# A graph network on one core: no memset between the scatters, and six of a tile's 13 layer-1 products between the groups of the next tile's aggregation

## The reference

```python
edge_index = jnp.stack([src, dst])
h = relu(layernorm(x));  x = x + L0(h, src, dst)
h = relu(layernorm(x));  x = x + L1(h, edge_index, edge_weight)

def L0(feat, W1, W2, b, src, dst):
    t1 = feat @ W1
    msg = t1[src] + feat[src] * feat[dst] @ W2
    scale = sqrt(out_deg[src]) * sqrt(out_deg[dst])
    agg = segment_sum(msg / scale[:, None], dst)
    embed = leaky_relu(where(in_cnt > 0, t1 + agg, 0) + b, 0.01)
    return embed / max(norm(embed), 1e-12)

def L1(h, edge_index, ew, W, b, W1, b1, W2, b2):
    # self-loops added; norm = dinv[row] * ew * dinv[col]
    h7 = segment_sum((h @ W)[col] * norm, row) + b
    return relu(h7 @ W1 + b1) @ W2 + b2
```

## Time and profile before

| | us |
|---|---|
| median of 3 runs | 2632.22 (2628.5 to 2633.63) |
| the profiled execution | 2630.78 |
| its span in the profile | 2628.8 |
| first scatter starts | 58.75 |
| last scatter starts | 1203.41 |
| layer 0's last step ends, about | 1754 |

### The profile page before, as it was taken

How to read it: one execution, slowest core, us unless ns; L and a number is a source line. 1 busy time by engine, 2 the same in 40 slices (tenths; PEclk the granted TensorE clock), 3 DMA queues, 4 the chain that set the end, 5 groups by cost and what they waited for, 6 DMA issues and landing times. The chain is left out here.

```text
span 2628.8 us, 22584 instructions
## 1 busy us (share of the span) xinstructions
PE 1912.9 (73%) x7229; PEld 1164.1 (44%) x7239; DVE 1340.5 (51%) x1970; ACT 483.5 (18%) x636; POOL 955.0 (36%) x1107
## 2 busy tenths in 40 slices
PE   5599477773211122113999999999998999999996
PEld 1388122551100011002777676757788534443443
DVE  7878588231000000002454545555665878787886
ACT  1000200331000000000555455534102400000000
POOL 2888888887777777772000000000000400000000
PEclk9755798886555555555999999999999999999998
DMA  7788600433002000010675767641774355565663
GB/s 287 313 337 331 239 8 8 143 109 101 1 1 88 1 13 1 26 62 13 230 268 215 269 217 272 224 167 53 261 231 132 102 154 164 166 182 156 176 174 114
DMA packets 338567, 394.90 MB, mean 150 GB/s; under 512 B 114000, under 2 KB 319674, under 8 KB 325563
## 3 DMA queue, kind: packets, MB, share of 16 engines
q1 hardware_dynamic: 219593, 306.93, 33.2%
q10 hardware_dynamic: 93110, 86.22, 10.1%
q0 software_dynamic: 25792, 0.88, 0.8%
HBM read 221.43 MB, written 172.51 MB: 150 GB/s over the span
## 5 line engine op out<-in xcount | busy, mean ns | idle before, releaser
L377 POOL DMA_INDIRECT table<-valT,idxT x806 | 831.0, 1031 | 227.8 <-issue 227.2
L789 PE MATMUL psum<-hx,region 128*128 128x257 f32 x1250 | 322.4, 407 | 300.4 <-issue 212.6
L2005 PE MATMUL psum<-wgt,big 128*65 128x384 f32 (+3 forms) x1600 | 529.8, 493 | 1.2 <-DVE wgt L1953 1.2
L1953 DVE SCALAR_TENSOR_TENSOR wgt<-ratio,l3q,fcj 128x768 f32<-128x768 f32 (+2 forms) x400 | 412.5, 1048 | 94.0 <-PE psum L2005 86.8
L789 PEld LDWEIGHTS psum<-hx,region 128*128 128x128 f32 x1250 | 243.1, 203 | 346.8 <-issue 221.6
L789 PE MATMUL psum<-region,g 128*128 128x512 f32 (+1 forms) x672 | 297.7, 586 | 103.1 <-issue 59.2
L592 DVE TENSOR_TENSOR big<-big,psum 128x512 f32<-128x512 f32 (+1 forms) x325 | 210.4, 665 | 281.6 <-remote 163.6
L2005 PEld LDWEIGHTS psum<-wgt,big 128*65 128x65 f32 x1600 | 219.6, 138 | 302.8 <-issue 298.9
L1000 POOL PARTITION_ALL_REDUCE edges<-edge x1 | 0.5, 517 | 860.2 <-DVEq L1369 860.2
L789 PEld LDWEIGHTS psum<-region,g 128*128 128x128 f32 x672 | 128.0, 203 | 242.4 <-issue 174.3
L731 ACT ACTIVATE region<-psum 128x512 f32<-128x512 f32 (+1 forms) x175 | 87.0, 549 | 701.2 <-remote 400.5
(11 more groups left out here) (218 smaller groups left out, 1662.9 us busy)
## 6 DMA issues: line engine op xcount, KB each, us to landing
table<-tk SPq DMA_DIRECT2D x25, 3200.0 KB
fcj<-counts SPq DMA_DIRECT2D x150, 384.0 KB, 3.5
tk<-table SPq DMA_DIRECT2D x25, 1664.0 KB
counts<-region ACTq DMA_DIRECT2D x25, 1600.0 KB
tk<-table SPq DMA_DIRECT2D x25, 1536.0 KB
fcj<-counts SPq DMA_DIRECT2D x50, 448.0 KB, 3.7
counts_t<-region ACTq DMA_DIRECT2D x25, 800.0 KB
counts_b<-region ACTq DMA_DIRECT2D x25, 800.0 KB
```

The lines of the kernel that those rows point to most:

```text
L377: eng.indirect_dma_start(out=table, out_offset=bass.IndirectOffsetOnAxis(idxT[:, c:c + 1], 0), in_=valT[:, c, :], in_offset=None).then_inc ...
L789: mm = lambda o, l, r_, st, sp: eng.matmul(o, l, r_, start=st, stop=sp, skip_group_check=True)
L1953: eng.scalar_tensor_tensor(out=wgt[:, n % NW, u, 0:w], in0=rb[:, 2 * i + u, t0 * P:t0 * P + w], scalar=qs[:, k, 2 * i + u:2 * i + u + 1], ...
L2005: last = eng.matmul(acc[p % 2][u][0:FW, b, 0:hi - lo], ftx[:, k, 2 * i + u, :], wgt[:, n % NW, u, lo:hi], start=k == 0, stop=k == NT - 1, ...
```

## The change

Two things are changed. On GpSimd the memsets, their waits and their buffer are gone; the scatters follow each other in all 806 columns. In the tile steps six (`EARLY`) of the 13 layer-1 products of tile k - 1 stand between the groups of tile k's aggregation: two each behind groups 3, 4 and 5. The seven others keep the pattern: 3, `turn_ab`, 2, `dense`, and now 2. On VectorE the six lifts stand before q. On ScalarE `wt` is made before the copies of groups 3 to 6 instead of between 4 and 5. In the last step the lifts that fill the gaps are numbered anew.

```diff
-                    if c < FIRST_CODE or LATER_CODE <= c < STEADY:
-                        if rests:
-                            eng.wait_ge(sem("rest"), rests)
-                        eng.memset(rest[:, :], 0.0).then_inc(sem("rest"), 1)
-                        rests += 1
                     eng.indirect_dma_start(out=table, ...
...
 # VectorE
                 if prev and cur:
                     eng.wait_ge(sem("wt"), prev[0] + 3)
                     itself(row(wt, prev[0]))
+                    for n in range(EARLY):
+                        lift(n)
...
-                    for n in range(5 if last else 13):
+                    for n in range(EARLY if cur else 0, EARLY + 2 if last else 13):
                         lift(n)
...
 # ScalarE
                     normal(prev[0], g1)
-                take(k, 3)
-                take(k, 4)
-                if prev:
                     eng.wait_ge(sem("ag"), 13 * prev[0] + 1)
                     eng.activation(wt, tk[:, prev[1], :, :, 1], ACT.Copy).then_inc(sem("wt"), 1)
-                take(k, 5)
-                take(k, 6)
+                for g in range(3, 7):
+                    take(k, g)
...
 # TensorE
                         if g + 3 < 7:
                             turn(k, s, g + 3)
+                        if prev and g in (3, 4, 5):
+                            if g == 3:
+                                eng.wait_ge(sem("g1"), prev[0] + 1)
+                                eng.wait_ge(sem("diag"), prev[0] + 1)
+                            gathered(range(2 * g - 6, 2 * g - 4))
...
                 if prev:
-                    gathered(range(0, 3))
+                    gathered(range(EARLY, EARLY + 3))
                 turn_ab()
                 if prev:
-                    gathered(range(3, 5))
+                    gathered(range(EARLY + 3, EARLY + 5))
                 dense()
                 if prev:
-                    gathered(range(5, 13))
+                    gathered(range(EARLY + 5, 13))
```

More of the change, by code:

```diff
@@ L35 @@
 NGS = -(-EC // GS)
+EARLY = 6
 GROWS = -(-GR * NGS // 8) * 8
 QB = -(-EC // P)
-FIRST_CODE, LATER_CODE, STEADY = 28, 112, 352
 assert NG * G == EC and P % GS == 0 and SH % SB == 0
@@ L257, in phase_edges_and_l0 @@
         g1 = buf("g1", [P, D])
-        rest = buf("rest", [P, 2 * P])
         st1, mv1 = buf("st1", [P, 6]), buf("mv1", [P, 2])
@@ L360, in finish @@
                 eng.sem_inc(sem("done"), 1)
-            late, rests = 20, 0
+            late = 20
             for g in range(NGS):
@@ L638, in step @@
                                              op0=ALU.mult, op1=ALU.add, accum_out=nrm[:, 0:1]).then_inc(sem("ss"), 1)
-                    fill(5, 6)
+                    fill(8, 9)
                     eng.wait_ge(sem("root"), k + 1)
@@ L654, in step @@
                     eng.sem_inc(sem("var1"), 1)
-                    fill(7, 8)
+                    fill(10)
                     eng.wait_ge(sem("sd1"), k + 1)
@@ L664, in step @@
                     eng.sem_inc(sem("ln1"), 1)
-                    fill(9, 10, 11, 12)
+                    fill(11, 12)
                     assert ch.n == begun + 13, ch.n - begun
@@ L860, in step, with gathered @@
             def step(cur, prev, last=False):
+                def gathered(chunks):
+                    j, z = prev
+                    of, g = (wt, g1) if cur else (tk[:, 0, :, :, 1], hk)
+                    for n in chunks:
+                        eng.wait_ge(sem("af"), 13 * j + max(n + 1, 3))
+                        if n < 12:
+                            mul = mm(pL[:, n % 3, :], g[:, n % 2 * P:n % 2 * P + P], of[:, 4 * (n // 2):4 * (n // 2) + 4, :], True, True)
+                        else:
+                            for o in range(2):
+                                mul = mm(pL[:, 0, o * P:o * P + P], g[:, o * P:o * P + P], of[:, NT - 1, :], True, True)
+                        mul.then_inc(sem("ag"), 1)
                 if cur:
@@ L873, in step @@
                             turn(k, s, g + 3)
-                    mul.then_inc(sem("q"), 1)
[L876 to L886, removed]
+                        if prev and g in (3, 4, 5):
[3 more added lines that the diff above has]
+                            gathered(range(2 * g - 6, 2 * g - 4))
+                    mul.then_inc(sem("q"), 1)
                 def turn_ab():
@@ L898, in dense @@
                     mul.then_inc(sem("e"), 1)
-                if prev:
+                if not cur:
                     eng.wait_ge(sem("g1"), prev[0] + 1)
                     eng.wait_ge(sem("diag"), prev[0] + 1)
-                if not cur:
                     gathered(range(13))
```

## The result

| | us | ratio to before |
|---|---|---|
| before, median of 4 | 2632.3 (2628.5 to 2633.63) | |
| after, median of 4 | 2851.8 (2818.14 to 2873.8) | 1.083 |
| after, the two executions that the next ratio goes by | 2818.14 and 2831.96 | 1.0735, 95% interval 1.0686 to 1.0783 |
| forecast | 2705 (2610 to 2950) | 1.028 |
| after, the profiled execution | 2818.14, span 2816.5 | |

Slower, as forecast and inside the range, but by 187 us from profiled execution to profiled execution (220 from median to median) where 73 were forecast. The ratio of 1.0735 and its interval leave out after's two slow executions (2871.62 and 2873.8, over 1.5% above its fastest), which the median of 4 has in it. That it lies inside the range doesn't bear the forecast's sum out; the next rows show where the time went.

What follows compares the result with a forecast made beforehand. Layer 0's end was taken as set by the scatters, then the tiles left on TensorE. Removing memsets +25.9 and early products +47.1 gave +73.0 us, 2705 us; range 2610 to 2950.

Steps and rivals of the forecast that it cites:

- The 2.80 us per operation: TensorE's pace beside scatters without memsets, read in the tile steps and applied from 466 us on.
- the tail: End of layer 0's scatters: TensorE stays slow for about 25 us after the last scatter.
- I take them as unchanged: Deduplication and degrees, until 466 us: VectorE sets the pace, so removing the memsets changes nothing there.
- the 53.6 us of earlier scatters: GpSimd in layer 0: without 268 memsets of 0.20 us each, scatters end at 1149.8 instead of 1203.4 us.
- three tiles more: End of layer 0: 22 tiles instead of 19 left to run at the fast rate, 26.83 us each.
- + 25.9: Cost in us of removing the memsets: three tiles of 26.83 less 54.6 of earlier start.
- part 1: Removing GpSimd's memsets in layer 0, forecast to cost 25.9 us.
- Rival 1: Deduplication also held back at 2.80 us per operation, 204 us a chunk: +329 us, 2961 us; chance 0.25.
- the tiles' own stores may begin the state: Tile steps, 466 to 610 us: stores may start TensorE's slow state, an argument against the deduplication being slowed too.
- Part 2: Six early products and ScalarE's new order in the tile steps: TensorE waits 2.14 us in each of 22 tiles, +47.1 us.
- A pause of 0.20 us is what lets TensorE report on time: Tile steps: 0.20 us more per scatter, from a memset, keeps TensorE's results from being reported late.
- rival 2: Memsets did nothing to TensorE's delay; scatters end 53.6 us earlier, -8.5 us in all, 2624 us; chance 0.15.

Runs made afterwards that it cites:

- e10: The kernel before without its 268 memsets, tile steps as before: 2741.34 us, ratio 1.051, beside the kernel before at 2605.28.
- e1: The kernel before without its 268 memsets, tile steps as before: 2077.07 us against 2120.71, ratio 0.979.
- e8: The changed kernel with ScalarE's old order (groups 3 and 4 copied before the layer-1 copy): 2779.97 us, ratio 1.068, beside the kernel before at 2603.62.
- e5: The changed kernel once more, on another chip: 2084.38 us against 2119.93 for the kernel before, ratio 0.984.
- e4: The kernel before, memsets kept, with the six early products, but ScalarE copying groups 3 and 4 before the layer-1 copy: 2123.32 us, ratio 1.001.
- e9: The kernel before with the full 128x256 memset before all 806 scatters: 2219.89 us against 2605.28, ratio 0.853.
- e7: The kernel before with a small 128x32 memset before all scatters: 2691.27 us against 2603.62, ratio 1.034.

## Why the prediction was right and wrong

**The stage and the quantity: right.** Layer 0's end is the last scatter and the tiles left behind it, and the loss was counted in these terms. The 2.80 us per operation is there again to a hundredth (204 us for 73), and so is the tail (28.0 us from the last scatter to abT at 1233.25; 28.5 before).

**The step that failed** is the sentence "I take them as unchanged", on the deduplication. It went by VectorE's pace in the earlier trace rows, which was read under memsets, and priced TensorE at 2.80 us only from 466 us on. e10 and the windows of after show that the deduplication is held back as well, at the same 2.80 us an operation. The degrees are not: their 806 products took 169 us in after and 168 before. Two terms of the sum fall with it: the 53.6 us of earlier scatters (GpSimd waits for columns, and the last scatter comes 1.8 us later instead), and three tiles more (it was five). Instead of + 25.9 part 1 cost 134.2 + 1.4 = 135.6. e10, part 1 alone in another session, measured + 136. It confirms the size and that part 1 is enough for the loss, but an agreement to the microsecond is luck: e10's executions lie up to 48 us apart, and its traced one finished its chunks and scatters later than after did. In a free session the same part gains 44 us (e1), so the + 135.6 holds for held sessions only.

**Rival 1 had the mechanism** and the price of a chunk, 204 us, but summed it to + 329. It took all chunks as fully held. Measured: chunk 1 was done at 165.1 and not at 263, the degrees at 357.0 and not at 431, chunk 2 took 97 us, chunk 3 131 and the last one 110. The chunks were done at 1103 instead of 1295. One reason is in the trace of after: where GpSimd has stood still long enough, TensorE keeps its pace for some 25 us after the scatters begin again, as it stays slow for 25 us after they end.

```profile
454.70:480.00 25.30, 17.68 (x44) 6.16 (x44) 19.36 (x11) 0.61 (x2) 19.21 (x21) 0.84 0.09 18
480.00:586.00 106.00, 18.58 (x29) 5.80 (x29) 11.91 (x15) 0.00 (x0) 79.64 (x83) 0.53 0.02 1
993.70:1020.00 26.30, 20.77 (x51) 7.16 (x52) 22.80 (x13) 0.00 (x0) 20.17 (x21) 0.85 0.02 2
1020.00:1103.00 83.00, 10.69 (x17) 3.62 (x18) 7.81 (x11) 0.00 (x0) 61.85 (x65) 0.53 0.02 1
```

44 and 51 operations pass in the first 25 us beside dense scatters, then 29 in 106 and 17 in 83 us. So the state builds up and drains; it isn't there from the first scatter on. But not every dry spell gives a free 25 us. In e8 GpSimd stood still for 27.5 us before its chunk 3 and for 24.9 us before its last one. Each time, the first scatter behind the dry spell and the 25 us from it:

```profile
451.67 0.96 POOL L371 DMA_INDIRECT table<-valT,idxT  x1 [27.52 <-DVEq L484]
987.00 0.96 POOL L371 DMA_INDIRECT table<-valT,idxT  x1 [24.86 <-DVEq L484]
```

```profile
451.70:476.70 25.00, 17.61 (x44) 6.11 (x44) 20.94 (x12) 0.61 (x2) 19.14 (x20) 0.86 0.09 18
987.00:1012.00 25.00, 10.38 (x20) 3.70 (x20) 9.03 (x5) 0.00 (x0) 19.14 (x20) 0.63 0.02 1
```

Behind the first 44 operations pass and the chunk takes 128 us; behind the second only 20, and the last chunk takes 187 us, not 110. e10 has the same pair (59.9 us dry, then a chunk of 127; 23.5 us dry, then one of 188). In these traces the state had drained after 27.5 us or more without a scatter and not after 24.9 us or less. The prediction's argument against rival 1, that the tiles' own stores may begin the state, is refuted: from 586 to 993 the DMA share is 0.03, and TensorE is held back.

**Part 2: right.** 28.97 us a tile forecast, 28.95 measured in most; one gap, before the fourth group, ended by ScalarE; the counts_b block under 1 us (0.35). The term came to 50.9 instead of 47.1 because 24 tiles and not 22 stood behind. What the prediction didn't price is the clock: that it falls behind some of the gaps added 5.3 us here, and in e5 it happens in ten tiles. e4 and e8 confirm the cause of the gap: in ScalarE's old order 28.25 us, and the rest of the gap is the diagonal's.

**"A pause of 0.20 us is what lets TensorE report on time": half right.** In held sessions memsets do it (e9), but the pace isn't what matters (e7: the same pace, half the delay). And in free sessions there is nothing to be let through. There the scatters' end bounds layer 0, and a gain as in rival 2 applies: the last scatter starts 49.7 us earlier (forecast 53.6) and the kernel gains 43.6 (e1). By the Trainium skill, page "SBUF — State Buffer", section "Who interferes with whom", TensorE waits for no one. The free sessions agree with it (1482 operations beside scatters 1.26 us apart). In the held ones TensorE is late beside the scatters all the same (73 operations in 204 us), though not by longer operations: its bursts run as usual and the reports come late, which that section, on ports, doesn't cover. The sign of the change hangs on the session: + 7% or - 1.6%. That the session of the result was held, like the one in which before was profiled, is no part of the prediction's reasoning; in a free one the forecast would have had the wrong sign.

## What to carry to other kernels

A pace read under a condition that the change removes is no evidence for the pace without it: the 2.80 us stood in the trace for one stage, and every other stage in which the same two engines work side by side should have been priced by it, or at least given a chance as large as the forecast's own. Where an engine is idle for "issue" while another does indirect DMAs, run the kernel before on several chips and at several times before tuning against it; a setting that is 5% slower in a free session (memset everywhere) was 15% faster in a held one, and of the six programs seen in both kinds the only one whose time hardly depended on the session (2229 and 2220 us). And a long copy placed ahead of a short one that frees a buffer costs the wait of the fullest engine in every round, and now and then its clock as well.

## What the runs showed of the hardware

- One and the same program has two durations, 2120 and 2604 to 2634 us, by session, with scatters of the same length and pace (0.96 us, 1.26 apart) and the same number of their DMA packets (25,792). In held sessions TensorE gets one operation through per 2.80 us beside back-to-back indirect DMAs of GpSimd, with VectorE and ScalarE busy for 5% of the time (before, 594 to 1203). The operations run in bursts; what waits for them starts late (604.96 after a burst that ended at 594.3).
- This state takes some 25 us to build up and to drain. In after, 44 and 51 operations pass in the first 25 us behind dry spells of 28.8 and 28.4 us; in e8 and e10 dry spells of 24.9 and 23.5 us gave nothing of the kind (20 operations in 25 us in e8).
- Behind an idle gap of TensorE of 1.8 to 2.1 us in an otherwise full stretch the granted clock fell to 1.2 GHz in three of after's 24 tiles and in ten of e5's, and eight operations then took up to 3.7 us instead of 2.0; behind gaps of 1.2 us it didn't (e4 from 494 to 1009, e8 from 1231 on).
- A memset of 0.15 us in the 0.30 us gap that GpSimd leaves between two scatters in any case hardly slows the scatters (1.269 us against 1.263 to 1.266), and more than doubles what TensorE gets through (204 to 95 us a chunk).
- A 128x256 memset of 0.33 us between two scatters costs 0.19 to 0.20 us of pace (268 of them 49.7 us, 538 of them 104.7 us).
